# A gated cross-attention and quantized feed-forward block: attention's weight jobs with four buffers, w_down turned by DMA, half of the magnitudes made a stage earlier

## The reference, cut to what matters

```python
x = x + tanh(g_xattn) * attention(layernorm(x), ctx, ctx, w_q, w_k, w_v, w_o)   # 4 x 1024 rows of 512, 64 keys, 16 heads
x = x + tanh(g_ffn) * ffn(layernorm(x), w_gate, w_up, w_down)

def ffn(x, w_gate, w_up, w_down):                  # 512 -> 1536 -> 512
    x = act_qdq(x)                                 # 16 bits, one scale from max|x| over the whole tensor
    up = act_qdq(x @ lpbq_dequant(w_up).T)         # lpbq: 4 bits, a scale for each 32 columns of a row
    gate = act_qdq(x @ lpbq_dequant(w_gate).T)
    sig = fixed_qdq_u16(sigmoid(gate))
    gate = act_qdq(gate * sig)
    o = act_qdq(gate * up)
    return o @ lpbq_dequant(w_down).T
```

## Time and profile before

| | us |
|---|---|
| median of 3 executions (lowest, highest) | 1346.55 (1345.92, 1348.36) |
| the profiled execution | 1344.37 |
| its span, first to last instruction | 1342.5 |
| PE busy | 1218.1 (91%) |
| DVE busy | 1001.7 (75%) |
| ACT busy | 672.2 (50%) |
| POOL busy | 291.6 (22%) |

### The profile page before, as it was taken

One profiled execution on the slowest core, in us unless ns is written; L12 is line 12 of the kernel. 1 busy time (PEld: TensorE's weight loads), 2 busy tenths in 40 slices (PEclk: granted clock), 3 DMA queues, 4 the chain that ended last, 5 costly groups with the idle time before them and its releaser, 6 DMA issues. The chain is left out here.

```text
span 1342.5 us, 18904 instructions
## 1 busy us (share of the span) xinstructions
PE 1218.1 (91%) x5937; PEld 593.9 (44%) x5937; DVE 1001.7 (75%) x1444; ACT 672.2 (50%) x782; POOL 291.6 (22%) x375
## 2 busy tenths in 40 slices
PE   7899899999899989999999999999980079999998
PEld 6644544544444444444444444444430034444443
DVE  2778789779777667777777699979999975555554
ACT  3534444444353334444443588857669963343341
POOL 0246435535534221111111222300210000000000
PEclk9999999999999999999999999999995589999999
DMA  9123523533434458787876899943389854454453
GB/s 333 35 53 106 140 84 84 140 94 98 124 91 130 139 195 227 239 257 233 244 214 205 292 329 339 328 140 132 133 274 340 300 181 142 164 182 162 163 176 106
DMA packets 187403, 246.64 MB, mean 184 GB/s; under 512 B 99280, under 2 KB 111568, under 8 KB 187344
## 3 DMA queue, kind: packets, MB, share of 16 engines
q1 hardware_dynamic: 187056, 245.95, 57.0%
q10 hardware_dynamic: 288, 0.00, 0.0%
HBM read 136.32 MB, written 91.23 MB: 169 GB/s over the span
## 5 line engine op out<-in xcount | busy, mean ns | idle before, releaser
L1414 PE MATMUL gpG<-xph,Wh 128*128 128x512 f16 x384 | 145.6, 379 | 1.4 <-DVE xpl L1329 1.4
L1937 PE MATMUL pD<-Wh,xph 128*128 128x512 f16 x384 | 145.5, 379 | 1.0 <-DVE xpl L1912 1.0
L1414 PE MATMUL gpG<-xpl,Wh 128*128 128x512 f16 x384 | 145.5, 379 | 0.0
L1414 PE MATMUL gpG<-xph,Wl 128*128 128x512 f16 x384 | 145.5, 379 | 0.0
L1414 PE MATMUL pU<-xph,Wh 128*128 128x512 f16 x384 | 145.5, 379 | 0.0
L1414 PE MATMUL pU<-xpl,Wh 128*128 128x512 f16 x384 | 145.5, 379 | 0.0
L1414 PE MATMUL pU<-xph,Wl 128*128 128x512 f16 x384 | 145.5, 379 | 0.0
L1937 PE MATMUL pD<-Wl,xph 128*128 128x512 f16 x384 | 145.5, 379 | 0.0
L1937 PE MATMUL pD<-Wh,xpl 128*128 128x512 f16 x384 | 145.5, 379 | 0.0
L1304 ACT ACTIVATE gst<-gpG,rw 128x512 f32<-128x512 f32 x96 | 65.7, 685 | 130.9 <-PE gpG L1414 103.2
L1342 DVE TENSOR_REDUCE gmx<-gst 128x512 f32 (+1 forms) x96 | 65.4, 682 | 56.6 <-ACT gst L1304 56.4
(11 more groups left out here) (248 smaller groups left out, 2615.5 us busy)
## 6 DMA issues: line engine op xcount, KB each, us to landing
dub<-up_d SPq DMA_DIRECT2D x42, 768.0 KB, 4.7
gate_d<-gst SPq DMA_DIRECT2D x96, 256.0 KB, 3.2
gb<-gate_d SPq DMA_DIRECT2D x24, 768.0 KB, 6.9
up_d<-ust SPq DMA_DIRECT2D x72, 256.0 KB, 5.0
eu<-up_d SPq DMA_DIRECT2D x22, 768.0 KB, 6.6
xr<-xn_d SPq DMA_DIRECT2D x9, 1024.0 KB, 6.4
xin<-in_x SPq DMA_DIRECT2D x32, 256.0 KB, 3.6
x_d<-x SPq DMA_DIRECT2D x32, 256.0 KB, 2.3
```

The source lines that it names most:

```text
L1414: mm = pe.matmul(ps[:, :], Ws[:, it, kt * P:(kt + 1) * P], xs[:, kt, :], start=(kt == 0 and Ws is Wh and xs is xh), stop=(kt == KT - 1 and ...
L1937: mm = pe.matmul(pD[4 * t + q][:, :], os_[n][:, cs], Ws[:, it, :], start=(it == 0 and os_ is oh and Ws is Wh), stop=(it == IT - 1 and os_ ...
```

## The change

It has three parts.

**Attention.** Jobs get four buffers instead of two (`w`, `q`, `d`, `lo`; `hi` keeps two), and other places in a step. `pjd` stays at delay 1 but moves behind the sums of its step on DVE. `pjhi` moves to delay 2, ahead of the exponentials on ACT. `pjlo` stays at delay 2 but moves on POOL behind `pr` and the division. The turn is at delay 3 and the store at delay 4.

```diff
-        J = Jobs(mk, ph, "pj", JB, 2, None, gate_stored)
+        J = Jobs(mk, ph, "pj", JB, JB, None, gate_stored, 2)
...
-                q = job_at(k, jobs, 2)
+                q = job_at(k, jobs, 3)
                 if q is not None:
                     sp.wait_ge(*at(J.lo_done, JB * b, q + 1))
...
                 q = job_at(k, jobs, 0)
                 if q is not None:
-                    job_divide(pool, J, b, q)
+                    job_divide(pool, J, b, q, q + 1)
+                q = job_at(k, jobs, 2)
+                if q is not None:
+                    pool.wait_ge(*at(J.hi_done, JB * b, q + 1))
+                    pool.wait_ge(*at(turn_in[q % 2], 16 * JB * b, 32 * (q // 2 - 1)))
+                    pool.tensor_tensor(J.lo[q][:, :], J.d[q][:, :], J.hi[q % 2][:, :], ALU.subtract).then_inc(J.lo_done, 1)
...
                 if have(k - 1):
                     sums(b, k - 1)
+                q = job_at(k, jobs, 1)
+                if q is not None:
+                    dve.wait_ge(*at(J.row_done, 5 * JB * b, 5 * q + 5))
+                    dve.wait_ge(*at(J.int_done, JB * b, q + 1))
+                    dve.wait_ge(*at(J.lo_done, JB * b, q - JB + 1))
+                    dve.tensor_tensor(blocks(J.d[q][:, :]), blocks(J.q[q][:, :]), spread(J.sn[:, q, :]), ALU.mult).then_inc(J.deq_done, 1)
```

```diff
                     if it in (5, 9, 11):
                         q = 3 * t + (5, 9, 11).index(it)
-                        if t:
-                            job_store(sp, J, i, q, job_dst(i, q))
-                        else:
...
+                        sp.wait_ge(*at(J.lo_done, JR * i, q + 1))
...
+                        for part, to in zip((J.hi[q], J.lo[q]), turned[q]):
+                            sp.dma_start_transpose(to[:, :].rearrange("p (k n) -> p k n", n=P), part[:, :]).then_inc(turn_in[q], 16)
+            turned_store(sp, i, JR - 1, job_dst(i, JR - 1))
+
+        def turned_store(sp, i, q, dsts):
+
+            sp.wait_ge(*at(turn_in[q], 32 * i, 32))
...
                         product(pe, pG[m % 3], Wh, Wl, xh[t], xl[t], it, ready).then_inc(g_ps, 1)
-                        if it % 4 == 3 and t:
-                            job_turn(pe, J, i, 3 * t + it // 4, ident)
```

```diff
+AWAY = range(0, QT, 2)
...
+        away = {(m // IT, m % IT): [k for k in range(QT, 2 * QT) if k - QT in AWAY and slot_of(k) + 3 == m] for m in range(FT * IT)}
...
+                    for k in away[j, it]:
+                        sp.wait_ge(f_done, k + 1)
+                        sp.dma_start(f_d[AWAY.index(k - QT), :, :], f_away).then_inc(f_out, 16)
...
+                    for k in away[j, it]:
+                        act.wait_ge(f_done, k + 1)
+                        act.activation(nq[:, k - QT, :], f_away, ACT.Abs).then_inc(f_abs, 1)
...
+                to = nq[:, k - QT, :]
+                if k - QT in AWAY:
+                    to, n = f_away, AWAY.index(k - QT)
+                    if n:
+                        dve.wait_ge(f_abs, n)
+                        dve.wait_ge(f_out, 16 * n)
...
+            stay = [k for k, g in enumerate(ORDER) if g not in AWAY]
+
             def signed(k):
-                return k == 0 or k % 3 == 2
+                return k in stay and stay.index(k) % 4 == 0
...
+                def load_f(g):
+                    n = AWAY.index(g)
+                    if n < 2:
+                        sp.wait_ge(xui_done, [k for k in range(QT) if k % NB == 2 + n][-1] + 1)
+                    else:
+                        sp.wait_ge(o_done, AWAY[n - 2] + 4)
+                    sp.dma_start(fr[n % 2], f_d[n, :, :]).then_inc(fr_in[n % 2], 16)
...
+                    if k not in stay:
+                        dve.wait_ge(f_abs, AWAY.index(g) + 1)
+                        largest(nq[:, g, :], nq[:, g, :], u, 1.0, pmx[:, n:n + 1], p_done)
+                        continue
```

More of the change, by code:

```diff
@@ L160, in flamingo_block @@
             d_unit = sb(ff, "d_unit", [P, H], F32)
-            x_row = [sb(ff, f"x_row{n}", [P, H], F32) for n in range(2)]
+            x_rows = sb(ff, "x_rows", [P, 2 * H], F32)
+            x_row = [x_rows[:, n * H:(n + 1) * H] for n in range(2)]
+            f_away = x_rows[:, :].bitcast(I16)[:, 0:I]
             load_w = [lambda eng, c, d=d, s=s: load_weights(eng, W, d, s, c) for d, s in zip(wsc, w_in)]
@@ L210, with __init__ @@
 class Jobs:
-    def __init__(self, mk, ph, tag, R, NJ, bank, stored=None):
+    def __init__(self, mk, ph, tag, R, NJ, bank, stored=None, NH=None):
         nc, sb, pb, sem, _ = mk
@@ L549, in _ @@
                 load_x(j)
-            for q in range(2):
+            for q in range(JB):
                 job_load(sp, J, 0, q, w_src[q, 0, :, :])
@@ L602, in _ @@
             schedule(sp, step)
-            for n in range(2):
-                sp.wait_ge(*at(J.loaded[n], 0, 16 * (12 // J.NJ + 1)))
+            for n in range(JB):
+                sp.wait_ge(*at(J.loaded[n], 0, 16 * (12 // JB + 1)))
         @block.gpsimd
@@ L1166, in gate_phase @@
         AHEAD = 5
-        J = Jobs(mk, ph, "gj", JR, NJ, [pb(ph, "gjbank")])
-        turned = [[sb(ph, f"gj{part}T{n}", [P, 512], F16) for part in ("hi", "lo")] for n in range(3)]
-        turn_in = [sem(f"gj_turn_in{n}", 32) for n in range(3)]
+        J = Jobs(mk, ph, "gj", JR, NJ, None)
+        turned = [[sb(ph, f"gj{part}T{n}", [P, 512], F16) for part in ("hi", "lo")] for n in range(JR)]
+        turn_in = [sem(f"gj_turn_in{n}", 32) for n in range(JR)]
         pG = [pb(ph, f"gpG{n}") for n in range(3)]
@@ L1428, in keep_warm, with up_phase @@
         pe.matmul(ps, words[:, 0:P], words.unsqueeze(1).to_broadcast([P, 2, 2 * P]), start=True, stop=True)
-def up_phase(mk, x_d, x_pair, first_u, early_u, late_g, late_st, unit, d_unit, scale, gate_out, last_m, gate_d, up_d, W, w_in, load_w,
+AWAY = range(0, QT, 2)
+def up_phase(mk, x_d, x_pair, first_u, early_u, late_g, late_st, f_away, f_d, unit, d_unit, scale, gate_out, last_m, gate_d, up_d, W, w_in, load_w,
              ident, nq, umx, fmx, sci, scu, S_X, cols, tmp):
@@ L1729, in down_phase @@
             fa = [sb(ph, "xfa0", [P, I], I16)[:, :], last_m[:, :].bitcast(I16)]
-            last_gated, (up_spilled, spills) = up_out
+            last_gated, (up_spilled, spills), f_out, f_abs = up_out
+            fr = [early_u[2 + n][:, 0:I // 2].bitcast(I16) for n in range(2)]
+            fr_in = [sem(f"d_f_in{n}") for n in range(2)]
             oq = fa
@@ L1744, in down_phase, with by_act @@
             block = ph.enter_context(nc.Block())
+            stay = [k for k, g in enumerate(ORDER) if g not in AWAY]
             def signed(k):
-                return k == 0 or k % 3 == 2
+                return k in stay and stay.index(k) % 4 == 0
+            def by_act(k):
+                return k in stay and not signed(k)
             def upto(k, of):
```

123 lines of the change are left out of this document (59 added, 64 removed).

## The result

| | before | changed |
|---|---|---|
| median of the executions, us | 1346.24 | 1364.09 |
| ratio, 95% interval | | 1.0132 (1.0114 to 1.0149) |
| span of the profiled execution, us | 1342.5 | 1362.7 |
| PE busy | 1218.1 | 1226.6 |
| DVE busy | 1001.7 | 991.0 |

What follows compares the result with a forecast made beforehand. PE, busy 91% of the span, was taken as the bound, with DVE full in the up stage and product pass. Terms -8 + 1.2 + 2.5 - 13 = -17.3 us gave 1329 us against the median; eight-in-ten range 1320 to 1339.

Steps and rivals of the forecast that it cites:

- Attention, forecast -8: Attention: PE's 15.6 us of waits for `pr` shrink as `pjlo` and `pjd` leave its path; ends -15.6 and 0.
- (B): Rival, attention: gives nothing because `pr`, `pjs` and `pjd` hold each other; 1337 us, chance 0.11.
- Gate stage, forecast +1.2: Gate stage: -5.2 for twelve turns off PE, +1 boundaries, +3.7 gap at the end, +1.7 clock; ends -3 and +6.
- The chain of 3.8 us at the stage's end: Gate stage's end: SP issues two turns, waits for landing, then stores; 3.8 us pass, adding 3.7 to PE's gap.
- the boundary of a loop body, 0.4 us each: Gate stage: at three loop-body boundaries SP's wait delays stores and evictions; 0.4 us each, up to 1.5, +1 taken.
- 3.4 us in hand: Gate stage boundaries: PE was read as about 3.4 us ahead, covering most of SP's 3.8 us delay.
- Rival (A): Gate stage: turns by DMA cost more, each boundary 1.5 to 2 us, the end 5 or more; 1335 us, chance 0.13.
- Up stage, forecast +2.5: Up stage's second half: added magnitudes fit on ACT, but late `f_away` stores delay DVE near the end; ends 0.5 and 5.
- rival (E): Up stage: slow landings of all `f_away` stores make DVE wait 15 times, 28 us; slower kernel, 1355 us, chance 0.05.
- Product pass, forecast -13: Product pass: DVE's instructions fall from 43 to 36 at 1.85 us each; transfers needing 345 GB/s keep up.
- Rival (C): Product pass: transfers bound it at 302 GB/s, so the gain is 4 and not 13; 1338 us, chance 0.11.
- Down stage: Down stage: `quantize` of even tiles reads `fr` loaded two tiles ahead, behind PE; 0 us.

Runs made afterwards that it cites:

- attn: Only the attention part of the change, against the kernel before: 1361.56 us, ratio 1.0100.
- attn_hi3: Attention part alone with three `hi` buffers instead of two, against the kernel before: 1337.75 us, ratio 0.9931.
- gate: Only the gate stage's part (w_down's jobs turned by DMA), against the kernel before: 1355.07 us, ratio 1.0057.
- away24: Up and down stages' part alone, twelve even tiles (0 to 22) through f_away instead of sixteen, against the kernel before: 1338.00 us, ratio 0.9938.
- gate_mix: Gate stage's part alone, job 5 still turned by PE and stored at once, jobs 3 and 4 by DMA, against the kernel before: 1344.01 us, ratio 0.9972.

## Why the prediction was wrong

**Attention, forecast -8, measured +13.5 (`attn`).** The step that failed is the sentence that ACT's `pjhi` "reads ... a `hi` whose turn is long over". The change gives four buffers to `w`, `q`, `d` and `lo`, and two to `hi`, as the diff and the text on the change both say; job 2 at step 7 needs `hi` of job 0, whose turn SP issues at step 6, behind the turns of the rows. I counted that `pjhi` stands ahead of the exponentials and priced it by its duration (7.6 us for 12, hidden), but not by the wait that it brings along, though one of 2.89 us was in the earlier trace rows; it measured 4.6 us once in each of the three batches and 2.4 to 3.3 a step later. PE's idle time grew by 10.7 us. The clock's fall behind these waits, for which the sum had nothing in attention, added 5.7 us in the whole change and 7.8 in `attn`. None of my rivals had it: (B), on DVE and POOL, ended at no gain. The rest of the term held: without that wait PE waits 8.4 us for `pr` (6 to 9 were forecast), the ratio of `attn_hi3` is -9.3 us, and DVE's step is 12.2 us ("about 12.0 to 12.4").

**Gate stage, forecast +1.2 with its ends at -3 and +6, measured 7.7 (`gate`).** The chain of 3.8 us at the stage's end was right to a tenth. The gap that it leaves was a little larger, 4.4 us more than before (4.9 in `gate`) for 3.7. Mis-sized was the boundary of a loop body, 0.4 us each: ACT stood up to 7.4 us for a store and then evicted three products in a row.

```profile
592.27 1.36 ACT L1311 ACTIVATE gst<-gpG,rw 128x512 f32<-128x512 f32 x2 [7.35 <-DMA gate_d<-gst]
```

PE had no 3.4 us in hand there: it waited 1.77 and 2.43 us at two boundaries of the whole change (the 4.2 of its list), 3.6 us in three waits in `gate`. The clock's fall at the stage's end came too, 1.8 us for the 1.7 forecast, and once more behind a boundary, which I had not counted. A stretch of the whole change:

```profile
655.00:665.00 10.00, 7.57 (x29) 2.93 (x27) 4.25 (x7) 2.06 (x3) 0.00 (x0) 0.83 0.85 254
```

In `gate`'s trace, -5.2 of turns, 4.3 of idle, 2.0 of clock, 4.9 at the end and 1.7 of clock behind it make 7.7. Rival (A) named the boundaries and the end, with 0.13, and its price, 6 over the sum or 7.2 in all, is near the 7.7.

**Up stage, forecast +2.5 with 5 as the upper end, measured 8.5.** The mechanism was right and the size off. One part was missed: I counted waits in the last 33 us only, and where DVE has 1.5% of slack a wait in mid-stage is not made good either. `away24` has waits in mid-stage only, 5.0 us, and 2.4 of them reach the end. The other was the landing: 6.5 us in the tail, where I took `up_d`'s 4.0, though `Wl`'s 6.2 for the same 384 KB stood beside it in the earlier trace rows and I kept it for rival (E) alone.

**Product pass, forecast -13, measured -15.2.** 36 instructions as counted; they take 1.77 us each and not 1.85. A start follows the last by 1.74 us where nothing is waited for. Inside a `signed` tile it is 2.01, 11 times before and 4 now, and ten steps of 1.89 that the pass before had are gone. Rival (C) did not come: 379 GB/s. That 345 GB/s would be reached was right. **Down stage**: 0, as forecast. Between the pass and the first product 1.0 us was added: the filler matmuls run on until 1105.6, 1.3 us behind the last maximum, which the sum had left out.

**The range.** Its lower side was taken for the likelier error. Its upper end came from rivals that each lose a gain; none but (E) lost more than the gain, and (E) had 0.05. An order change that puts a wait for a DMA ahead of the engine's work on the path should have had a rival of its own: three batches, two steps each, 3 to 5 us.

## What to carry to other kernels

When an instruction moves ahead of work on the critical path, price its waits and not its duration: list every semaphore that it waits for, find for each the buffer count that sets it, and count the steps between the release and the wait. With buffers of a chain raised from two to four, the one left at two decides. A turn or store by DMA takes work off an engine for nothing only if the queue has something else to do until it lands; the last one of a loop body had not, and here the engine was cheaper. Where an engine is nearly full to the end of a stage, a wait anywhere in that stage is paid at its end, in these runs from half of it to all. And look at the granted clock behind each new wait of PE: in attention its fall cost 5.7 us on top of 10.7 us of waiting.

## What the runs showed of the hardware

The granted clock at the gate stage's start fell to the lower level in twelve of the seventeen programs and stayed in five, with nearly the same PE rows ahead of it: idle for 1.63 us, four filler matmuls, then a wait for `xpl`. A stretch of 10 us there in the whole change, and in `gate`, where it stayed:

```profile
505.00:515.00 10.00, 8.21 (x24) 2.95 (x25) 6.87 (x16) 4.25 (x7) 1.32 (x2) 0.66 0.68 213
```

```profile
490.00:500.00 10.00, 7.96 (x36) 3.34 (x37) 7.39 (x18) 5.62 (x10) 2.12 (x3) 1.00 0.74 223
```

Counted from the filler matmuls to the 61st product, the fall costs 0.3 to 2.6 us, mostly 1 to 2. All eleven programs with attention's part are among the twelve, so there it goes with that part, and a little of what attention's ratio shows may be this; why, no run shows. The twelfth is `gate_mix`, whose edit changes nothing ahead of this place. So 1 to 2 us between two such programs need not come from what their edits do. And transfers of up from DRAM ran at 379 GB/s for 67 us, with the 16 engines busy 95.7%.
